# Row sums of y squared: from TensorE products to ScalarE squares and VectorE sums in a two-layer graph kernel

## The reference, cut to what matters

```python
x = _layernorm(x + _L0_gnn_ref(x, adj, ...))      # y is what stands in the brackets, centred
# L1: deg = adj.sum(axis=0) + 1; dinv = rsqrt(deg)
xw  = x @ W
z   = dinv[:, None] * xw
out = relu(dinv[:, None] * (adj.T @ z + z) + b)
x   = _layernorm(x + out)
# _layernorm: (x - mean) / sqrt(var + 1e-5), over the 64 features
```

## Time and profile before

| | us |
|---|---|
| median of 3 runs (lowest, highest) | 641.5 (639.92, 642.29) |
| profiled execution, its own time | 641.78 |
| span of that execution | 640.1 |
| TensorE busy, share of span | 600.1, 94% |
| VectorE / ScalarE / GpSimd busy | 334.5 / 138.8 / 108.4 |

### The profile page before, as it was taken

One profiled execution on the slowest core, in us unless ns is written; L12 is line 12 of the kernel. 1 busy time (PEld: TensorE's weight loads), 2 busy tenths in 40 slices (PEclk: granted clock), 3 DMA queues, 4 the chain that ended last, 5 costly groups with the idle time before them and its releaser, 6 DMA issues.

```text
span 640.1 us, 10729 instructions
## 1 busy us (share of the span) xinstructions
PE 600.1 (94%) x4785; PEld 235.2 (37%) x4785; DVE 334.5 (52%) x355; ACT 138.8 (22%) x208; POOL 108.4 (17%) x126
## 2 busy tenths in 40 slices
PE   6989999999999999999999999999999999978775
PEld 5433333333333333333333335554343434313112
DVE  3789467768767776876675782644140402103004
ACT  2015060421506042150605117311000101001001
POOL 3006051240705122050503104100000000000000
PEclk9989999999999999999999999999999999999998
DMA  7998299959778694977879497699999999999991
GB/s 256 387 377 291 98 363 377 388 189 351 269 268 298 240 387 163 372 266 259 290 256 387 150 387 266 244 349 338 383 409 410 410 411 409 412 409 410 412 396 63
DMA packets 86002, 204.82 MB, mean 320 GB/s; under 512 B 4539, under 2 KB 7099, under 8 KB 85957
## 3 DMA queue, kind: packets, MB, share of 16 engines
q1 hardware_dynamic: 84196, 202.77, 85.1%
q10 hardware_dynamic: 1760, 1.38, 0.6%
HBM read 202.82 MB, written 1.31 MB: 319 GB/s over the span
## 4 chain that ended last, share of the span: by engine, by line
PE 76%; DMA 14%; DVE 7%; POOL 1%; ACT 1%; issue 1%; SPq 0%; ACTq 0%; DVEq 0%; POOLq 0%
PE psum L751 28%; PE psum L861 21%; PE psum L954 12%; DMA slot<-in_adj_dram 9%; PE psum L869 6%; DMA last_slot<-in_adj_dram 4%; DVE slot L583 3%; PE psum L795 2%; PE psum L745 2%; PE psum L974 1%; POOL turned L354 1%; DVE turn L562 1%; PE psum L722 1%; PE psum L934 1%; PE psum L922 1%; DVE last_slot L583 1%
## 5 line engine op out<-in xcount | busy, mean ns | idle before, releaser
L583 DVE STREAM_TRANSPOSE slot<-slot 128x2048 f32<-128x2048 f32 x80 | 177.7, 2279 | 75.9 <-PE psum L751 75.9
L751 PE MATMUL psum<-slot,E 128*64 128x512 f32 x768 | 173.8, 603 | 3.0 <-DVE slot L589 2.6
L861 PE MATMUL psum<-slot,T 32*64 32x512 f32 x2560 | 142.5, 590 | 0.0
L354 POOL COPY turned<-last_slot 32x1024 f32<-32x1024 f32 x80 | 84.4, 1055 | 285.8 <-DVE last_slot L583 281.5
L954 PE MATMUL psum<-slot,E 128*64 128x512 f32 x512 | 115.0, 596 | 10.5 <-DMA slot<-in_adj_dram 9.7
L751 PEld LDWEIGHTS psum<-slot,E 128*64 128x64 f32 x768 | 53.2, 138 | 114.4 <-issue 113.4
L404 ACT ACTIVATE turned<-last_slot 32x1024 f32<-32x1024 f32 x80 | 84.3, 1054 | 40.6 <-DVE last_slot L583 38.9
L861 PEld LDWEIGHTS psum<-slot,T 32*64 32x64 f32 x2560 | 55.9, 132 | 84.4 <-issue 84.4
L694 DVE TENSOR_TENSOR T<-psum,dinv 128x256 f32<-128x256 f32 x10 | 4.2, 425 | 144.1 <-PE psum L974 143.7
L395 ACT ACTIVATE T<-T 32x256 f32<-32x256 f32 x60 | 24.8, 414 | 224.1 <-DVE T L567 222.9
L954 PEld LDWEIGHTS psum<-slot,E 128*64 128x64 f32 x512 | 35.2, 137 | 86.5 <-issue 60.0
(11 more groups left out here) (110 smaller groups left out, 268.4 us busy)
## 6 DMA issues: line engine op xcount, KB each, us to landing
slot<-in_adj_dram SPq DMA_DIRECT2D x152, 1024.0 KB, 14.3
last_slot<-in_adj_dram SPq DMA_DIRECT2D x30, 1024.0 KB, 7.7
turned<-in_adj_dram SPq DMA_DIRECT2D x10, 1024.0 KB, 15.1
X<-in_x_dram SPq DMA_DIRECT2D x5, 256.0 KB, 5.1
out_dram<-T ACTq DMA_DIRECT2D x10, 128.0 KB, 5.8
T<-in_L_gnn_W_u_dram ACTq DMA_DIRECT2D x2, 16.0 KB, 2.9
T<-in_L_gnn_W_i_dram ACTq DMA_DIRECT2D x2, 16.0 KB, 4.6
beta_b<-in_L_gnn_ln_beta_dram SPq DMA_DIRECT2D x1, 32.0 KB, 11.5
```

The source lines that it names most:

```text
L354: nc.gpsimd.tensor_copy(turned[c * Q32:(c + 1) * Q32, a].rearrange("p h k j r -> p (h k j) r"), last_blocks[a * Q32:(a + 1) * Q32, :, c, : ...
L583: v.transpose(parts, parts).then_inc(chunk_cut, 1)
L751: return mm(acc[half[b % 2], :], E[:, b, :], view[:, b % CB, :], start=(b < 2), stop=(b >= NB - 2))
L861: last = mm(acc[half[h], a, :], T[step % 2][rows_a, jb, (c - a) % 4, :], slot[step % 2][rows_a, h:NF:2, :, cols], start=False, stop=False, ...
```

## The change

The squares of y no longer come from the transposed y in PSUM but from X itself, row by row; and the sums over the features no longer come from TensorE but from a VectorE reduction into `rsum`. GpSimd's scaling of X also waits for `y_turned`, as X is still read by the transposes. The order lists of all three engines change with it.

```diff
-        yy = after[:, JW:2 * JW]
+        yy = after[:, JW:2 * JW].rearrange("p (b f) -> p b f", f=F)
...
                 pool.wait_ge(rstd_ready, g + 1)
+                pool.wait_ge(y_turned, g + 1)
...
+            def square_y(g):
+                act.wait_ge(y_ready, g + 1)
+                if g >= 1:
+                    act.wait_ge(y_summed, g)
+                nc.scalar.activation(yy, X[:, g * GB:(g + 1) * GB, :], ACT.Square).then_inc(yy_ready, 1)
...
             def copy_yT(g):
                 act.wait_ge(y_turned, g + 1)
-                nc.scalar.activation(yy, y_turn, ACT.Square).then_inc(yy_ready, 1)
...
-                nc.scalar.activation(std_y[g % 2][:, :], sums[:, 1, :], ACT.Sqrt, bias=eps_col[:, 0:1],
+                nc.scalar.activation(std_y[g % 2][:, :], rsum[:, :], ACT.Sqrt, bias=eps_col[:, 0:1],
...
+            def sum_y(g):
+                dve.wait_ge(yy_ready, g + 1)
+                if g >= 1:
+                    dve.wait_ge(std_y_ready, g)
+                v.tensor_reduce(rsum[:, :], yy, AX, ALU.add).then_inc(y_summed, 1)
...
             restore(0)
             norm_h(0)
+            sum_y(0)
             norm_h(1)
             restore(1)
             make_group(0)
+            sum_y(1)
             restore(2)
             make_group(1)
             norm_h(2)
+            sum_y(2)
             restore(3)
             make_group(2)
             norm_h(3)
+            sum_y(3)
             restore(4)
+            make_group(3)
             norm_h(4)
-            make_group(3)
+            sum_y(4)
             restore(5)
+            make_group(4)
             restore(6)
-            make_group(4)
             restore(7)
...
-            def sum_y(g):
-
-                pe.wait_ge(yy_ready, g + 1)
-                wait_sums_read()
-                for i in range(GB // 2):
-                    last = mm(sums[:, 1, 2 * i:2 * i + 2], yy[:, i * P:(i + 1) * P], pairs[:, :], start=True, stop=True)
-                last.then_inc(y_summed, 1)
```

More of the change, by code:

```diff
@@ L122, in build @@
         h_turn = [bank[5 + i].rearrange("p (b f) -> p b f", f=F) for i in range(2)]
-        sums = bank[7][:, 0:2 * GB].rearrange("p (w b) -> p w b", w=2)
+        sums = bank[7][:, 0:GB]
         o_turn = [bank[4 + i][:, 0:JB * F].rearrange("p (b f) -> p b f", f=F) for i in range(2)]
@@ L437, in root_h @@
                     act.wait_ge(h_read, g - 1)
-                nc.scalar.activation(std_h[g % 2][:, :], sums[:, 0, :], ACT.Sqrt, bias=eps_col[:, 0:1],
+                nc.scalar.activation(std_h[g % 2][:, :], sums, ACT.Sqrt, bias=eps_col[:, 0:1],
                                      scale=1.0 / F).then_inc(std_h_ready, 1)
+            def square_y(g):
[3 more added lines that the diff above has]
+                nc.scalar.activation(yy, X[:, g * GB:(g + 1) * GB, :], ACT.Square).then_inc(yy_ready, 1)
             def copy_yT(g):
                 act.wait_ge(y_turned, g + 1)
[L443 to L446, removed]
-                nc.scalar.activation(yy, y_turn, ACT.Square).then_inc(yy_ready, 1)
                 if g >= 1:
@@ L467, in _ @@
             root_h(1)
+            square_y(0)
             copy_yT(0)
             root_y(0)
+            square_y(1)
             copy_yT(1)
@@ L474, in _ @@
             square_h(4)
+            square_y(2)
             copy_yT(2)
@@ L477, in _ @@
             root_h(3)
+            square_y(3)
             copy_yT(3)
+            root_y(3)
             root_h(4)
-            root_y(3)
+            square_y(4)
             copy_yT(4)
@@ L819, in turn_h @@
                 last.then_inc(h_turned, 1)
-            read = {"h": 0, "y": 0, "last": "h"}
-            def wait_sums_read():
-                pe.wait_ge(std_h_ready if read["last"] == "h" else std_y_ready, read[read["last"]])
             def sum_h(g):
@@ L832, in sum_h @@
                 else:
-                    wait_sums_read()
+                    pe.wait_ge(std_h_ready, g)
                 for k in range(CB):
-                    last = mm(sums[:, 0, :].rearrange("p (h k) -> p k h", k=CB)[:, k], hh[g][:, k * P:(k + 1) * P],
+                    last = mm(sums.rearrange("p (h k) -> p k h", k=CB)[:, k], hh[g][:, k * P:(k + 1) * P],
                               pairs[:, :], start=True, stop=True)
                 last.then_inc(h_summed, 1)
-                read.update(h=g + 1, last="h")
             def t_pairs(step, lo, hi):
@@ L915, in turn_y @@
                 transpose_rows(y_turn, g).then_inc(y_turned, 1)
-            def sum_y(g):
-                pe.wait_ge(yy_ready, g + 1)
-                wait_sums_read()
-                for i in range(GB // 2):
-                    last = mm(sums[:, 1, 2 * i:2 * i + 2], yy[:, i * P:(i + 1) * P], pairs[:, :], start=True, stop=True)
-                last.then_inc(y_summed, 1)
-                read.update(y=g + 1, last="y")
             def project_y(g):
@@ L1000, in _ @@
             last_products(range(2, JB)).then_inc(h_done, 1)
-            sum_y(0)
             project_y(0)
@@ L1004, in _ @@
             first_round(2)
-            sum_y(1)
             project_y(1)
@@ L1011, in _ @@
             first_round(2)
-            sum_y(2)
             project_y(2)
@@ L1020, in _ @@
             first_round(2)
-            sum_y(3)
             project_y(3)
@@ L1025, in _ @@
             first_round(2)
-            sum_y(4)
             project_y(4)
```

## The result

| | before | changed |
|---|---|---|
| median of 6 runs each (lowest, highest), us | 641.03 (639.75, 642.29) | 646.61 (644.88, 647.7) |
| ratio to before, 95% interval | | 1.0083 (1.0063, 1.0103) |
| profiled execution, own time / span, us | 641.78 / 640.1 | 647.70 / 646.0 |
| TensorE / VectorE / ScalarE busy, us | 600.1 / 334.5 / 138.8 | 598.4 / 337.3 / 139.2 |

The change makes the kernel slower by 0.83%, 5.6 us; 646.8 had been forecast. The profiled execution of the changed kernel is the slowest of its six. The six times lie in two groups: three of 644.9 to 645.8 us with a mean granted clock of 0.991 or 0.992, and three of 647.4 to 647.7 us with 0.982 to 0.986, the profiled one among them; the median lies between, where no run does.

A forecast was written before the change was run, and what follows sets the result against it. The load stream, started in earnest by the y stage, was taken to bound the kernel. 641.8 + 2.4 (order) + 2.9 (clock) = 647.1 us profiled, 646.8 for the median; range 643.5 to 650.

The forecast's parts named there:

- What bounds: Whole kernel: the stream of loads sets the end, and the y stage sets when that stream starts in earnest.
- Place 1: First z: the sum delays norm_h(1); first sweep at 407.65, 1.04 us later, paid back by 0.98 us of saved matmuls.
- Places 2 and 3: Sixth to eighth transposes, now later in VectorE's list: TensorE idles 4.4 us ahead of m = 11, 3.2 ahead of m = 14.
- The order's share: Y stage: the changed order alone, summed over three places, costs 2.4 us, without any fall of the clock.
- place 3: Seventh and eighth transposes: m = 15 starts at 453.65 instead of 451.18, TensorE leaves 2.45 us later; +1.3 us net.
- nearly a microsecond of the whole: Up to about 455 us, a microsecond won or lost by TensorE counts almost fully in the total; later nothing.
- the stream hides it: Rival, y-stage loads: DMA engines already busy, later issues only find a shorter queue, nothing lost, 641.5 us; chance 0.06.
- The clock's share: Behind the 4.4 us idle time ahead of m = 11: one fall to half clock, costing 2.9 us.
- rival of two: Rival: the 3.2 us gap ahead of m = 14 also brings a fall, worth 2 to 3 us, 649.5; chance 0.27.
- One fall only in the trace: Argument for the rival without a fall: the old trace showed one, at one gap; 644.2 us, chance 0.2.

The follow-up runs named there:

- the version with all idle times filled: Changed kernel plus unused 128 x 128 matmuls in TensorE's three idle times (8 ahead of the first sweep, 16 of m = 11, 12 of m = 14): 642.89 us, ratio 1.0024.
- the two versions with early transposes: VectorE's list rewritten, transposes placed where VectorE waits for TensorE: on the changed kernel 636.15 us, ratio 0.9931; on the kernel before, without sums, 638.66 us, ratio 0.9952.
- the early version: Changed kernel with VectorE's list rewritten, sum_y(0) behind norm_h(1) and each transpose where VectorE waits for TensorE: 636.15 us, ratio 0.9931.

## Why the prediction was right, point by point

- **What bounds.** The loads end 5.9 us later, and the whole is 5.9 us longer in the profiled executions (647.70 - 641.78). SyncE issues m = 16 6.4 us later (461.26 against 454.87), so the stream of loads passed on nine tenths of the y stage's loss.
- **Place 1.** First sweep at 407.73, with the stage 0.27 us late in this execution: 407.46, where 407.65 was worked out. The square took 0.63 us, as taken, and the reduction 0.69 where 0.64 had been taken. The page "VectorE: DVE Perf Modes" of the Trainium skill (Rules for kernel authors) calls the reduction the slowest operation; here it took what its neighbours of 128 x 512 took, 0.69 us, and the measurement decides. That it stands on the path is what costs.
- **Places 2 and 3.** Idle 4.24 and 3.16 us, foretold 4.4 and 3.2. Without the clock, m = 15 at 453.62, foretold 453.65.
- **The order's share, 2.4 us: too large.** By the version with all idle times filled it is 0.24% (0.13 to 0.35), 1.5 us (0.8 to 2.2), the lower end of the bounds or under it. (Its terms as written add up to 2.5; place 3 has 2.45 for m = 15.) The delay up to the loads came as worked out: in that version SyncE issues m = 16 at 457.30, 2.4 us later than at 454.87. What was off is "nearly a microsecond of the whole": its loads end at 605.74 + 18.48 = 624.22, only 1.0 us later than 623.24. The issue of m = 16 in the changed kernel and then in that version:

```profile
461.26 2.08 SPq L302 DMA_DIRECT2D last_slot<-in_adj_dram  x2
```

```profile
457.30 2.08 SPq L302 DMA_DIRECT2D last_slot<-in_adj_dram  x2
```

  The time from issue to landing tells where 1.4 us went. Of the kernel before, for the loads of m = 16 and 17, and then of that version:

```profile
DMA to landing us min/median/max: 8.3/8.7/9.2
```

```profile
DMA to landing us min/median/max: 6.9/7.3/7.7
```

  A load issued later found a shorter queue. This is the rival "the stream hides it", in part. The changed kernel itself, which issues m = 16 another four microseconds later, at 461.26, has 8.8 us again and passed on nearly all of its loss. The other profiled executions bear out the link, with scatter: where these loads landed in 7.3 to 7.7 us (three executions), the loads ended 166.9 to 167.2 us behind the issue of m = 16; with 8.3 to 9.1 us (seven, the kernel before among them) 167.1 to 168.4; with 11.0 and 11.4 us, in the two versions with early transposes, 169.1 and 170.1. What makes the queue shorter in one execution than in another was not tried, so the share that the stream hides is known only roughly.
- **The clock's share, 2.9 us: the right size, but not from one fall.** It is 3.8 us (1.0083 - 1.0024 = 0.0059 of 641); by the intervals of the two 2.3 to 5.3, which holds the 2.9. The profiled execution has two falls. Behind m = 11 the work up to the end of project_y(4) took 451.27 - 441.31 = 9.96 us, and 448.27 - 441.06 = 7.21 with the idle times filled: 2.8 us, the forecast's 2.9. Behind m = 14, the 48 matmuls up to the end of the first round took 11.96 us against 462.42 - 451.42 = 11.0: 1.0 us more. The forecast gave a second fall a chance of 0.27 since 3.2 us is hardly more than 2.80; but the clock fell behind the 3.16 us in each of the six profiled executions that have that idle time. So what the forecast had wrong is the number of falls: its rival of two happened, in the profiled execution at a lower price than the 2 to 3 us it was given. The price varies: 1.0 us also in two other versions, 1.2 in the kernel before with the changed order, and 2.4 in the two versions in which only one idle time was filled (13.4 against 11.0). The Trainium skill's page "TensorE: Matmul & The Clock Gate" (Why this matters for your kernels) warns of such gaps, and its warning holds for the 3.2 us as well as for the 4.4, which the forecast did not draw from it; the trace agrees for 3.16 us and more, and in part for 2.16 to 2.86.
- "One fall only in the trace" left out that the clock is below its full level again at 636 to 640 us (0.57 in the mean), and that near 7 us TensorE had waited 2.74 us for a DMA in the kernel before with no fall behind it. The rows showed waits for VectorE alone.
- The two errors, 0.9 us too much for the order and 0.9 us too little for the clock, cancel. Also, the median of 646.61 lies between two groups of runs near 645.4 and 647.5. That the sum came within 0.2 us of it is luck; what held is the order's delay up to the loads, the idle times, and that the clock costs more than the order.

Here are the chains behind the comparison of the clock's share, of the changed kernel and then of the version with the idle times filled (start us, us, what):

```profile
446.04 4.13 PE psum L770 x16
450.17 1.10 PE psum L937 x8
...
454.42 11.96 PE psum L770 x48
```

```profile
441.06 1.94 PE psum L770 x8
...
447.17 1.10 PE psum L937 x8
...
453.62 8.80 PE psum L770 x40
462.42 3.43 PE psum L957 x16
...
605.74 18.48 DMA last_slot<-in_adj_dram
```

## What to carry to other kernels

When work moves from one engine to another, its cost is where it stands in the new engine's list, not its duration: with five reductions of 0.69 us the kernel was 0.2 or 0.7% faster, or 5.6 us slower together with what they were allowed to push back. Look in the old trace for the times in which the receiving engine waits, and put the independent work (here the transposes) there, ahead of the chain that others wait for. And count TensorE's new idle times: each of more than some 2 us may be followed by a stretch at half the clock, which here cost more (3.8 us) than the later order itself (1.5 us).

## What the runs showed of the hardware

- In the y stage, after an idle time of 3.16 us or more TensorE's clock was at 1.2 GHz in every profiled execution (ten idle times in six executions). After 2.16 us it had fallen in two of four, after 2.57 in one of one (16 sweep matmuls took 5.35 us against 3.65), after 2.86 it had not. After 1.64 and 1.30 us it never had. Near 43 us it fell behind 2.24 to 2.80 us in eight executions and did not behind 1.96 to 2.19 in four. Near 7 us TensorE had waited 2.6 to 3.1 us for a DMA in all twelve, and the clock stayed at 1.00 from 6 to 11 us. So between 2.2 and 3.1 us the length of an idle time does not settle it.
- The same fall does not always cost the same: behind 3.16 us the 16 sweep matmuls of m = 14 and 15 took 5.09, 5.35 or 6.5 to 6.6 us, against 3.65 us at the full clock.
- A matmul of 128 x 128 in f32 that nobody needs took 0.23 us, and 36 of them in idle times made the kernel 3.8 us faster (2.3 to 5.3).
- At 440 to 445 us the kernel before moved 318 GB/s and the early version 414, at a DMA share of 0.96 and 1.03: the share hardly tells a stream that waits for its issues from one at its full rate, the GB/s and the time to landing do.
